# The last FFN of a two-layer kernel: two batches per product of 512 columns, high parts by ScalarE, and the first transposes ahead of the last shared step

## The chip, the cores and the metric

The kernel runs on one core of a Trainium2 chip. The metric is the device time of one execution in microseconds (us); the median of three runs is quoted, and beside it stands one profiled execution, from which every row below comes.

## The reference, cut to what matters

Two layers of cross attention and FFN act on `x` of 4 batches x 256 tokens x 256. The change touches the last FFN, and the order of work at the seam between the mixture-of-experts FFN of the first layer and the attention of the second.

```python
x = x + L0_xattn(layernorm(x), ctx, ...)
x = x + L0_ffn(layernorm(x), ...)              # experts + 0.2 * shared FFN
x = x + L1_xattn(ctx, ctx, masks, layernorm(x), ...)
# L1_ffn on layernorm(x); the weights are lut[idx]
gate = einsum('bsh,oh->bso', x, lut[gate_idx]) # 256 -> 688
up   = einsum('bsh,oh->bso', x, lut[up_idx])   # 256 -> 688
h    = silu(gate) * up
out  = einsum('bsh,oh->bso', h, lut[down_idx]) # 688 -> 256
```

All of it is float32. The kernel gets there on TensorE by splitting both factors in a high and a low part of type fp32r and summing three products (high x high, low x high, high x low).

## The kernel before, in words

Five engines run instruction lists of their own (`@block.tensor` PE, `@block.scalar` ACT, `@block.vector` DVE, `@block.gpsimd` POOL, `@block.sync` SP for DMA), written out by hand in order, and tied by semaphores. Each engine takes its own list strictly in order, so a wait holds up all that stands behind it.

Most of the time goes to ten "units" (the shared FFN in two halves of tokens and eight experts). A unit has nine steps; in each, `first` (L729) makes 6 products into a bank of `hb`, ScalarE applies gelu, and `second` (L748) adds float32 products into `yb` two steps later. The last unit, E + 1, is the second half of the shared FFN; its last two `second` steps stand after the unit.

Then comes the last FFN, the stage of the change. 688 hidden rows are NG = 6 tiles (five of 128, the last of 48, for which gate and up share one product). The four batches of 256 tokens are taken one after another, so that there are 24 tiles n = b * NG + f. The parts are:

- `transpose_x3(b)` (PE, L847): 4 transposes of the normalised rows `xn` into `tb`. It waits for `x3n_ok`. `x3T_copy(b)` (ACT, helper line L902) makes `xT_hi`, and `x3T_split(b)` (DVE, L1519) makes `xT_lo`.
- `gate_up(b, f)` (PE, L868): 6 gate and 6 up products of 256 columns into the two halves of one of four banks (GRING = 4); 6 for the last tile. It waits until the products of the tile four before are taken from the bank (`prod_ok`).
- silu (ACT, L1111 or L1113) of the gate half into `gate_of(r)`.
- two DVE instructions: L1541 writes gate * up as fp32r (`h_hi`), and L1542 writes the same product as float32. POOL (L547) subtracts the two into `h_lo`.
- `down(b, f)` (PE, L883): 6 products of 256 columns into a bank for the batch, three tiles behind gate_up (GLAG = 3).
- `finish(b)` (DVE, L1526) adds the bank to `x`; SP sends the batch to `out`.

Between these tiles the lists of ACT, DVE and POOL carry what is left of the attention for batches 2 and 3 (and the end of batch 1): `combined(b)` (DVE statistics, L1126), `inv_std(3, b)` (POOL, L440 and L433), `attend(b)` (DVE, L1446 to L1457), `exps(1, b)` (ACT, L922, with a change of ScalarE's table to exp and back to silu), `add_probs(1, b, 4)` (DVE, L1272, L1275, L1126), `inv_std(4, b)` (POOL) and `norm_x(4, b)` (DVE, L1132), which releases transpose_x3(b). `add_shared(1)` (DVE, L1431) adds the shared FFN's banks to the tokens of batches 2 and 3, so nothing of these can start before the last `second`.

Of the kernel before, what the change touches and what calls it, by code (L numbers as in the profile page):

```python
# [25 lines left out]
P = 128  # L26
# [22 lines left out]
GRING, GLAG = 4, 3  # L49
# [12 lines left out]
def program(nc, t):  # L62
    xbuf = t["xbuf"]
    ctx = ExitStack()
    with ctx:
# [47 lines left out]
        h_hi = sb("h_hi", [P, GRING, S], F32R)  # L113
        h_lo = sb("h_lo", [P, GRING, S], F32R)
# [59 lines left out]
        ffn_banks = (hb[0], hb[1], hb[2], yb[1])  # L174
# [102 lines left out]
        prod_ok = sem("prod_ok")  # L277
        g_lo_ok = sem("g_lo_ok")
# [138 lines left out]
        def _(gp):  # L417
# [124 lines left out]
            inv_std(4, 0, 1e-5)  # L542

            for n in range(B * NG):
                gp.wait_ge(prod_ok, n + 1)
                r = n % GRING
                gp.tensor_tensor(h_lo[:, r, 0:S], product(r), h_hi[:, r, 0:S].bitcast(F32), ALU.subtract)\  # L547
                    .then_inc(g_lo_ok, 1)
                if n == 0:
                    inv_std(4, 1, 1e-5)  # L550
                elif n == 2:
                    inv_std(3, 2, 1e-5)
                elif n == 5:
                    inv_std(3, 3, 1e-5)
                elif n == 7:
                    inv_std(4, 2, 1e-5)
                elif n == 13:
                    inv_std(4, 3, 1e-5)
# [3 lines left out]
        def _(pe):  # L562
# [272 lines left out]
            for s in range(STEPS - LAG, STEPS):  # L835
                second(E + 1, s, True, 1)

# [13 lines left out]
            def gate_up(b, f):  # L851
                n = b * NG + f
                if n < GRING:
                    if n == GRING - 1:
                        pe.wait_ge(shared_read, 4)
                    pe.wait_ge(h32_ok, UNITS * NF)
                    pe.wait_ge(low_ok, UNITS)
                else:
                    pe.wait_ge(prod_ok, n - GRING + 1)
                if f == 0:  # L860
                    pe.wait_ge(x3T_lo, b + 1)
                last = f == NG - 1
                for part, first_col in enumerate((BOTH0,) if last else (GATE0, UP0)):
                    terms = [(w, a, k) for k in range(DK)
                             for w, a in ((gw_hi, xT_hi), (gw_lo, xT_hi), (gw_hi, xT_lo))]
                    for i, (w, a, k) in enumerate(terms):
                        at = first_col + (k * P if last else k * FULL + f * P)
                        mm = pe.matmul(ffn_banks[n % GRING][:, part * S:(part + 1) * S], w[:, at:at + P],  # L868
                                       a[:, b % 2, k, 0:S], start=(i == 0), stop=(i == len(terms) - 1))
                mm.then_inc(gu_mm, 1)  # L870

            def down(b, f):
                n = b * NG + f
                if n == NG:
                    pe.wait_ge(shared_read, 4)
# [11 lines left out]

            pe.wait_ge(lk, JOBS * JOPS)
            transpose_x3(0)
            for n in range(B * NG + GLAG):  # L890
                if n < B * NG:
                    gate_up(n // NG, n % NG)
                if n >= GLAG:
                    down((n - GLAG) // NG, (n - GLAG) % NG)
                if n % NG == 4 and n // NG + 1 < B:
                    transpose_x3(n // NG + 1)
# [3 lines left out]
        def _(act):  # L900
# [194 lines left out]
            def x3T_copy(b):  # L1095
                act.wait_ge(x3T_mm, b + 1)
                if b >= 2:
                    act.wait_ge(gu_mm, (b - 1) * NG)
                copy(xT_hi[:, b % 2, :, 0:S], tb[b % 2][:, :].rearrange("p (k s) -> p k s", k=DK)).then_inc(x3T_hi, 1)

            x3T_copy(0)
            for n in range(B * NG):
                b, f = n // NG, n % NG
                if n == 6:
                    exps(1, 2)
                elif n == 12:
                    exps(1, 3)
                act.wait_ge(gu_mm, n + 1)
                bank = ffn_banks[n % GRING]
                if f < NG - 1:  # L1110
                    act.activation(gate_of(n % GRING), bank[:, 0:S], ACT.Silu).then_inc(silu_ok, 1)  # L1111
                else:
                    act.activation(gate_of(n % GRING)[0:LASTG, :], bank[H:H + LASTG, 0:S], ACT.Silu).then_inc(silu_ok, 1)  # L1113
                if f == 4 and b + 1 < B:
                    x3T_copy(b + 1)
# [3 lines left out]
        def _(dve):  # L1119
# [392 lines left out]
            unit(E + 1, 1, shared=True, extra=tail)  # L1512
            norm_x(4, 0, x3n_ok)
            add_probs(1, 1, 4, (0,))


            def x3T_split(b):
                dve.wait_ge(x3T_hi, b + 1)
                dve.tensor_tensor(xT_lo[:, b % 2, :, 0:S], tb[b % 2][:, :].rearrange("p (k s) -> p k s", k=DK),  # L1519
                                  xT_hi[:, b % 2, :, 0:S].bitcast(F32), ALU.subtract).then_inc(x3T_lo, 1)  # L1520

            def finish(b):

                dve.wait_ge(down_mm, (b + 1) * NG)
# [8 lines left out]
            for n in range(B * NG):  # L1533
                b, f = n // NG, n % NG
# [91 lines left out]
```

## Time and profile before

| what | us |
|---|---|
| median of 3 runs | 323.04 (321.94 to 325.26) |
| profiled execution, its own time | 322.0 |
| its span | 320.1 |
| PE busy | 301.6 (94%) |
| DVE busy | 239.3 (75%) |
| ACT busy | 153.8 (48%) |
| POOL busy | 104.3 (33%) |

Rows give the start of an instruction in the span, its duration, the engine, the line, the operation, what it writes and reads, and in brackets how long the engine sat idle before and who ended that. Matmuls overlap, so the distance of their starts, and not the duration of one, is what one costs.

### The profile page before, as it was taken

The page shows a single profiled execution, that of the slowest core. Times are in us where ns is not written, and L with a number is a line of the kernel's source. Part 1 is how long each engine was busy: PE and PEld are TensorE (multiplying, and loading weights), DVE is VectorE, ACT ScalarE, POOL GpSimd, SP SyncE. Part 2 cuts the span into 40 slices and gives each one's busy share as a digit, 9 for nine tenths or more (in the row PEclk, how much of TensorE's full clock was granted, in tenths as well). Part 3 has the DMA queues.
Part 4 walks back from the last instruction along what each step waited for, and adds up shares of the span by engine and source line. Part 5 has one row for each costly group of instructions (what it writes and reads, how often), then busy time and mean ns, then how long its engine had stood idle before and what let it go on. Part 6 is the DMA issues. An engine that isn't in the chain of part 4 may idle for free.

```text
span 320.1 us, 5956 instructions
## 1 busy us (share of the span) xinstructions
PE 301.6 (94%) x1913; PEld 257.7 (80%) x1913; DVE 239.3 (75%) x649; ACT 153.8 (48%) x366; POOL 104.3 (33%) x146
## 2 busy tenths in 40 slices
PE   7998779997999999999999999999999979989895
PEld 4654557774989899898989989889888869979795
DVE  4758695602499989898998989899885748796742
ACT  2376473631346465554556555455641833634210
POOL 7327127670000605023060503305052206442432
PEclk9699789999899999999999999999999999999998
DMA  7993114825167574929466492927125000000101
GB/s 223 379 268 74 46 49 121 294 99 158 42 191 246 134 235 80 334 52 273 136 159 204 91 321 58 286 78 187 54 30 143 3 0 2 0 33 2 35 1 66
DMA packets 26258, 41.51 MB, mean 130 GB/s; under 512 B 3898, under 2 KB 16955, under 8 KB 26236
## 3 DMA queue, kind: packets, MB, share of 16 engines
q1 hardware_dynamic: 22012, 36.49, 35.8%
q0 software_dynamic: 4224, 4.75, 8.4%
q8 instruction: 11, 0.18, 0.2%
q14 instruction: 11, 0.09, 0.1%
HBM read 31.40 MB, written 9.82 MB: 129 GB/s over the span
## 4 chain that ended last, share of the span: by engine, by line
PE 83%; DVE 10%; DMA 2%; issue 2%; POOL 2%; SPq 1%; ACT 1%; DVEq 0%; POOLq 0%
PE hb L729 28%; PE yb L748 25%; PE hb L868 8%; PE yb L762 5%; PE tb L660 3%; PE rb L883 3%; PE yb L883 3%; PE yb L868 2%; PE rb L651 1%; POOL rstd L433 1%; DMA projw<-projw_dram 1%; DVE xT_lo L1288 1%; DVE x L1275 1%; PE yb L605 1%; DVE xn L1132 1%
## 5 line engine op out<-in xcount | busy, mean ns | idle before, releaser
L748 PE MATMUL yb<-raw,h 128*128 128x256 f32 x384 | 97.8, 385 | 0.0
L1031 ACT ACTIVATE h<-hb,b 128x320 f32<-128x320 f32 (+1 forms) x80 | 44.6, 559 | 69.9 <-PE hb L729 67.9
L748 PEld LDWEIGHTS yb<-raw,h 128*128 128x128 f32 x384 | 71.0, 194 | 7.6 <-ACT h L1031 0.3
L729 PE MATMUL hb<-xT_hi,w_hi 128*128 128x320 f32 (+1 forms) x180 | 72.4, 402 | 3.3 <-ACT small L1035 1.8
L531 POOL DMA_INDIRECT xacc_dram<-ysb,slot_i x16 | 25.0, 1565 | 126.0 <-ACT ysb L902 123.6
L729 PE MATMUL hb<-xT_lo,w_hi 128*128 128x320 f32 (+1 forms) x180 | 59.5, 331 | 0.0
L729 PE MATMUL hb<-xT_hi,w_lo 128*128 128x320 f32 (+1 forms) x180 | 59.3, 330 | 0.0
L1465 DVE TENSOR_TENSOR w_lo<-raw,w_hi 128x256 fp32r<-128x256 f32 x84 | 34.6, 416 | 17.2 <-ACT w_hi L902 17.1
L1158 DVE COPY_PREDICATED pick<-bits,pick 128x544 int32<-128x544 uint8 x56 | 43.2, 772 | 0.6
L729 PEld LDWEIGHTS hb<-xT_hi,w_hi 128*128 128x128 f32 x180 | 34.4, 191 | 8.9 <-issue 4.3
L729 PEld LDWEIGHTS hb<-xT_hi,w_lo 128*128 128x128 f32 x180 | 34.5, 192 | 2.6
L902 ACT ACTIVATE w_hi<-raw 128x256 fp32r<-128x256 f32 x90 | 36.5, 407 | 0.1
L729 PEld LDWEIGHTS hb<-xT_lo,w_hi 128*128 128x128 f32 x180 | 34.4, 191 | 1.7
L1154 DVE TENSOR_SCALAR pick<-bit,lut_x,lut 128x544 int32<-128x544 int32 x64 | 35.8, 580 | 0.0
L547 POOL TENSOR_TENSOR h_lo<-h,h_hi 128x256 fp32r<-128x256 f32 x24 | 17.7, 742 | 31.9 <-DVE h L1542 31.9
L868 PE MATMUL hb<-xT_hi,gw_hi 128*128 128x256 f32 x68 | 19.6, 288 | 2.9 <-DVE xT_lo L1519 2.8
L1288 DVE TENSOR_TENSOR xT_lo<-tb,xT_hi 128x320 fp32r<-128x320 f32 (+1 forms) x22 | 11.0, 540 | 15.0 <-ACT xT_hi L902 15.0
L868 PE MATMUL hb<-xT_lo,gw_hi 128*128 128x256 f32 x68 | 18.9, 278 | 0.0
L868 PE MATMUL hb<-xT_hi,gw_lo 128*128 128x256 f32 x68 | 18.9, 278 | 0.0
L902 ACT ACTIVATE xT_hi<-tb 128x320 fp32r<-128x320 f32 (+1 forms) x26 | 11.7, 496 | 14.9 <-PE tb L847 8.4
L511 POOL DMA_INDIRECT xbuf_dram<-xn,put_i x16 | 16.1, 1006 | 5.7 <-issue 4.5
L1126 DVE BATCH_NORM_STATS2 bst<-x 128x6 f32<-128x256 f32 x32 | 13.3, 416 | 6.1 <-DMA x<-xacc_dram 2.9
(216 smaller groups left out, 522.5 us busy)
## 6 DMA issues: line engine op xcount, KB each, us to landing
raw<-w1pack_dram SPq DMA_DIRECT2D x30, 384.0 KB, 3.5
raw<-w2pack_dram SPq DMA_DIRECT2D x30, 384.0 KB, 5.2
xbuf_dram<-h SPq DMA_DIRECT2D x8, 323.8 KB, 9.5
idx<-idx_dram SPq DMA_DIRECT2D x8, 272.0 KB, 6.0
xg<-xbuf_dram SPq DMA_DIRECT2D x8, 259.0 KB, 6.0
x<-x_dram SPq DMA_DIRECT2D x4, 256.0 KB, 4.5
xacc_dram<-x SPq DMA_DIRECT2D x2, 512.0 KB, 8.8
x<-xacc_dram SPq DMA_DIRECT2D x4, 256.0 KB, 4.0
```

The lines of the kernel that those rows point to most:

```text
L511: gp.indirect_dma_start(rows, bass.IndirectOffsetOnAxis(ap=put_i[:, tile, k:k + 1], axis=0), xn[:, tile, :], None, bounds_check=E * SLOTS ...
L531: gp.indirect_dma_start(t["xacc"], bass.IndirectOffsetOnAxis(ap=slot_i[:, u % 3, c:c + 1], axis=0), ysb[:, c, :], None, compute_op=ALU.add ...
L547: gp.tensor_tensor(h_lo[:, r, 0:S], product(r), h_hi[:, r, 0:S].bitcast(F32), ALU.subtract)\
L729: mm = pe.matmul(hb[s % RING][:, 0:n], w[:, s, k * P:(k + 1) * P], a[:, turn, k, 0:n], start=(i == 0), stop=(i == len(terms) - 1))
L748: mm = pe.matmul(yb[c // 2][:, (c % 2) * D:(c % 2 + 1) * D], h, w, start=(s == 0 and c % 2 == 0), stop=(s == STEPS - 1), skip_group_check= ...
L868: mm = pe.matmul(ffn_banks[n % GRING][:, part * S:(part + 1) * S], w[:, at:at + P], a[:, b % 2, k, 0:S], start=(i == 0), stop=(i == len(te ...
L883: mm = pe.matmul(down_banks[b % 2][:, i * D:(i + 1) * D], h[0:K, n % GRING, i * P:(i + 1) * P], w[0:K, at:at + D], start=(f == 0 and i == ...
L902: return act.activation(dst, src, ACT.Copy, scale=scale)
L1031: act.activation(hidden(s - 1, shared, turn), bank[:, 0:n], ACT.Gelu, bias=b1[:, expert, s - 1:s])\
L1154: dve.tensor_scalar(dst, bit0[:, :], lut_x[:, n:n + 1], lut_i[:, 2 * n:2 * n + 1], ALU.bitwise_and, ALU.bitwise_xor).then_inc(lk, 1)
L1158: dve.copy_predicated(dst, m, src).then_inc(lk, 1)
L1465: dve.tensor_tensor(w_lo[:, slot, :], raw1[:, slot, :], w_hi[:, slot, :].bitcast(F32), ALU.subtract)\
```

## The change

Batches are taken in two pairs. In each pair the f-th tile of both batches is one group g of 12 (g = pair * 6 + f); gate products go to one bank and up products to another, two banks each, with 512 columns (2 batches x 256). The group f = 0 still makes products of 256 columns, first those of the even batch, then those of the odd one. The tiles n = 0 to 23 now alternate between the batches of a pair. DVE makes the product once, in float32; its fp32r copy is made by ScalarE (`product_hi`). `h_hi` and `h_lo` now lie in the memory of `w_hi` and `w_lo`, in a ring of six. `down` follows two groups behind. `transpose_x3(0)` stands ahead of the last `second` of the shared FFN and `transpose_x3(1)` right behind it; those of batches 2 and 3 stand behind the down products of g = 4 and g = 5. DVE's order at the seam changes, and so do the places of the attention's remaining pieces.

In the diff, cut to its core, a chain of `if n == ...` is written as `n == 0: ...`, and `...` marks what is left out.

```diff
-GRING, GLAG = 4, 3
+GRING, GLAG = 6, 2
+PAIRS, HALVES = B // 2, 2 * NG
-        ffn_banks = (hb[0], hb[1], hb[2], yb[1])
+        gate_banks, up_banks = (hb[0], hb[2]), (hb[1], yb[1])
+        h_hi, h_lo = w_hi, w_lo
 @@ POOL
+            inv_std(4, 1, 1e-5)
+            for n in range(PAIRS * HALVES):
+                gp.wait_ge(g_hi_ok, n + 1)
+                h_lo[n % 6] = product - h_hi          (gp.tensor_tensor, then g_lo_ok)
+                n == 1: inv_std(3, 2)   n == 3: inv_std(3, 3)
+                n == 6: inv_std(4, 2)   n == 9: inv_std(4, 3)
 @@ PE
+            def gate_up(g):
+                p, f = g // NG, g % NG
+                if g < 2:
+                    pe.wait_ge(h32_ok, UNITS * NF)
+                    pe.wait_ge(low_ok, UNITS)
+                    if g == 1:
+                        pe.wait_ge(shared_read, 4)
+                else:
+                    pe.wait_ge(prod_ok, 2 * g - 2)
+                for cols in (slice(0, S), slice(S, 2 * S)) if f == 0 else (slice(0, 2 * S),):
+                    if f == 0:
+                        pe.wait_ge(x3T_lo, 2 * p + 1 + cols.start // S)
+                    for bank, first_col in ((gate_banks[g % 2], BOTH0),) if last else ((gate_banks[g % 2], GATE0),
+                                                                                       (up_banks[g % 2], UP0)):
+                        for i, (w, a, k) in enumerate(terms):
+                            at = first_col + (k * P if last else k * FULL + f * P)
+                            mm = pe.matmul(bank[:, cols], w[:, at:at + P], a[:, p, k, cols],
+                                           start=(i == 0), stop=(i == len(terms) - 1))
+            for s in range(STEPS - LAG, STEPS - 1):
+                second(E + 1, s, True, 1)
+            transpose_x3(0)
+            second(E + 1, STEPS - 1, True, 1)
+            transpose_x3(1)
             pe.wait_ge(lk, JOBS * JOPS)
+            for g in range(PAIRS * NG + GLAG):
+                if g < PAIRS * NG:
+                    gate_up(g)
+                if g >= GLAG:
+                    down(2 * (g - GLAG))
+                    down(2 * (g - GLAG) + 1)
+                if g in (4, 5):
+                    transpose_x3(g - 2)
 @@ ACT
+            def product_hi(n):
+                act.wait_ge(prod_ok, n + 1)
+                if n >= GRING:
+                    act.wait_ge(down_mm, n - GRING + 1)
+                copy(h_hi[0:K, r, :], product(r)[0:K, :]).then_inc(g_hi_ok, 1)
+            x3T_copy(0)
+            x3T_copy(1)
+            for n in range(0, PAIRS * HALVES, 2):
+                if n == 4:
+                    exps(1, 2)
+                elif n == 8:
+                    exps(1, 3)
+                silu(n)
+                silu(n + 1)
+                product_hi(n)
+                product_hi(n + 1)
+                if n in (8, 10):
+                    x3T_copy(n // 2 - 2)
 @@ DVE
-            norm_x(4, 0, x3n_ok)
             add_probs(1, 1, 4, (0,))
+            norm_x(4, 0, x3n_ok)
+            add_probs(1, 1, 4, (1,))
+            norm_x(4, 1, x3n_ok)
+            x3T_split(0)
             for later in range(2, B):
                 dve.wait_ge(x_back[later], 16)
             add_shared(1)
-            x3T_split(0)
+            x3T_split(1)
+            for n in range(PAIRS * HALVES):
+                dve.wait_ge(silu_ok, n + 1)
-                dve.tensor_tensor(h_hi[0:K, r, 0:S], gate_of(r)[0:K, :], up, ALU.mult)
                 dve.tensor_tensor(product(r)[0:K, :], gate_of(r)[0:K, :], up, ALU.mult).then_inc(prod_ok, 1)
+                n == 0: combined(2)        n == 1: attend(2)
+                n == 2: combined(3)        n == 3: attend(3)
+                n == 5: add_probs(1, 2, 4) n == 7: norm_x(4, 2, x3n_ok)
+                n == 8: add_probs(1, 3, 4) n == 9: x3T_split(2)
+                n == 10: norm_x(4, 3, x3n_ok)
+                n == 11: x3T_split(3)
+                n == 15: finish(0), finish(1)
+            finish(2)
+            finish(3)
```

## Rows read from the trace of the kernel before

**Rows 1.** The page: granted clock in 40 slices of 8 us, and the chain's shares.
```profile
PEclk9699789999899999999999999999999999999998
...
PE 83%; DVE 10%; DMA 2%; issue 2%; POOL 2%; SPq 1%; ACT 1%; DVEq 0%; POOLq 0%
```

**Rows 2.** Chain that ended last, 250 us on: start us, us, what.
```profile
249.91 1.40 PE hb L729 x6
...
259.95 1.29 DVE x L1431 x2
...
261.98 4.33 PE hb L868 x36
...
287.12 1.65 PE hb L868 x12
...
304.26 1.38 PE yb L868 x12
305.64 0.71 PE rb L883 x6
...
316.81 0.69 DVE x L1526
```

**Rows 3.** Instructions of DVE in order of time, 256 to 284 us.
```profile
256.17 0.73 DVE L1132 TENSOR_SCALAR xn<-x,mv,rstd 128x256 f32<-128x256 f32 x2 [1.13 <-POOL rstd L433]
...
264.05 0.42 DVE L1541 TENSOR_TENSOR h_hi<-h,hb 128x256 fp32r<-128x256 f32 x1 [2.21 <-ACT h L1111]
264.39 0.41 DVE L1542 TENSOR_TENSOR h<-h,hb 128x256 f32<-128x256 f32 x1
...
268.74 0.41 DVE L1126 BATCH_NORM_STATS2 bst<-x 128x6 f32<-128x256 f32 x1
...
269.81 0.39 DVE L1541 TENSOR_TENSOR h_hi<-h,yb 128x256 fp32r<-128x256 f32 x1
...
272.21 1.00 DVE L1446 SCALAR_TENSOR_TENSOR xg<-x,mv,scores 128x256 f32<-128x256 f32 x2
...
274.83 0.41 DVE L1541 TENSOR_TENSOR h_hi<-h,hb 48x256 fp32r<-48x256 f32 x1
...
279.26 0.16 DVE L1272 RECIPROCAL rsum<-esum 128x2 f32<-128x2 f32 x1
...
282.11 0.40 DVE L1541 TENSOR_TENSOR h_hi<-h,hb 128x256 fp32r<-128x256 f32 x1
...
283.33 1.13 DVE L1132 TENSOR_SCALAR xn<-x,mv,rstd 128x256 f32<-128x256 f32 x2 [0.48 <-POOL rstd L433]
```

**Rows 4.** Instructions of ACT in order of time, 263 to 293 us.
```profile
263.63 0.38 ACT L1111 ACTIVATE h<-hb 128x256 f32<-128x256 f32 x1 [1.46 <-PE hb L868]
...
274.93 0.60 ACT L922 ACTIVATE xg<-xg,nmx,rstd 128x256 f32<-128x256 f32 x1 [1.57 <-DVE nmx L1457]
...
276.22 1.28 ACT L1111 ACT_TABLE_LOAD   x1
...
292.30 1.07 ACT L1111 ACTIVATE h<-hb 128x256 f32<-128x256 f32 x3
```

**Rows 5.** The page: ScalarE's copies of 128x256 to fp32r, mean ns.
```profile
L902 ACT ACTIVATE w_hi<-raw 128x256 fp32r<-128x256 f32 x90 | 36.5, 407 | 0.1
```

**Rows 6.** Instructions of POOL in order of time, 278 to 283 us.
```profile
278.76 1.42 POOL L547 TENSOR_TENSOR h_lo<-h,h_hi 128x256 fp32r<-128x256 f32 x2 [1.01 <-DVE h L1542]
282.29 0.22 POOL L440 TENSOR_SCALAR vare<-mv 128x2 f32<-128x2 f32 x1 [2.10 <-DVE mv L1129]
```

**Rows 7.** Instructions of PE in order of time that began after idle time.
```profile
34.13 0.71 PE L676 MATMUL rb<-xT_hi,gate_parts 128*128 128x512 f32 x2 [2.65 <-DVE xT_lo L1288]
...
284.51 0.66 PE L847 MATMUL tb<-ident,xn 128*128 128x128 f32 x4 [0.97 <-DVE xn L1132]
```

**Rows 8.** Windows: stretch, length, busy (x) of PE, PEld, DVE, ACT, POOL, clock, DMA, GB/s.
```profile
34.00:36.00 2.00, 1.87 (x6) 1.51 (x7) 1.75 (x8) 0.33 (x1) 0.00 (x0) 0.70 0.00 0
36.00:38.00 2.00, 2.00 (x6) 1.18 (x4) 0.00 (x0) 1.86 (x7) 1.36 (x2) 0.50 0.00 0
```

More of the change, by code:

```diff
@@ L542, in _ @@
             inv_std(4, 0, 1e-5)
-            for n in range(B * NG):
-                gp.wait_ge(prod_ok, n + 1)
+            inv_std(4, 1, 1e-5)
+            for n in range(PAIRS * HALVES):
+                gp.wait_ge(g_hi_ok, n + 1)
                 r = n % GRING
-                gp.tensor_tensor(h_lo[:, r, 0:S], product(r), h_hi[:, r, 0:S].bitcast(F32), ALU.subtract)\
+                gp.tensor_tensor(h_lo[:, r, :], product(r), h_hi[:, r, :].bitcast(F32), ALU.subtract)\
                     .then_inc(g_lo_ok, 1)
-                if n == 0:
-                    inv_std(4, 1, 1e-5)
-                elif n == 2:
+                if n == 1:
                     inv_std(3, 2, 1e-5)
-                elif n == 5:
+                elif n == 3:
                     inv_std(3, 3, 1e-5)
-                elif n == 7:
+                elif n == 6:
                     inv_std(4, 2, 1e-5)
-                elif n == 13:
+                elif n == 9:
                     inv_std(4, 3, 1e-5)
@@ L862, in gate_up @@
                 last = f == NG - 1
[L863 to L869, printed above, removed]
+                for cols in (slice(0, S), slice(S, 2 * S)) if f == 0 else (slice(0, 2 * S),):
[3 more added lines that the diff above has]
+                                                                                       (up_banks[g % 2], UP0)):
+                        terms = [(w, a, k) for k in range(DK)
+                                 for w, a in ((gw_hi, xT_hi), (gw_lo, xT_hi), (gw_hi, xT_lo))]
+                        for i, (w, a, k) in enumerate(terms):
+                            at = first_col + (k * P if last else k * FULL + f * P)
+                            mm = pe.matmul(bank[:, cols], w[:, at:at + P], a[:, p, k, cols],
+                                           start=(i == 0), stop=(i == len(terms) - 1))
@@ L870, in gate_up, with down @@
                 mm.then_inc(gu_mm, 1)
[L872 to L874 removed]
+            def down(n):
+                b, f = n // HALVES * 2 + n % 2, n // 2 % NG
+                if n == 1:
                     pe.wait_ge(shared_read, 4)
@@ L1542, in _ @@
                 dve.tensor_tensor(product(r)[0:K, :], gate_of(r)[0:K, :], up, ALU.mult).then_inc(prod_ok, 1)
-                if f == 4 and b + 1 < B:
-                    x3T_split(b + 1)
                 if n == 0:
-                    add_probs(1, 1, 4, (1,))
-                elif n == 1:
-                    norm_x(4, 1, x3n_ok)
-                elif n == 2:
                     dve.wait_ge(shared_read, 4)
                     combined(2)
-                elif n == 4:
+                elif n == 1:
@@ L1553, in _ @@
                     attend(2)
+                elif n == 2:
+                    combined(3)
+                elif n == 3:
+                    attend(3)
                 elif n == 5:
-                    combined(3)
+                    add_probs(1, 2, 4)
                 elif n == 7:
-                    add_probs(1, 2, 4)
+                    norm_x(4, 2, x3n_ok)
                 elif n == 8:
-                    norm_x(4, 2, x3n_ok)
+                    add_probs(1, 3, 4)
+                elif n == 9:
+                    x3T_split(2)
@@ L1560, in _ @@
                 elif n == 10:
-                    attend(3)
-                elif n == 13:
-                    add_probs(1, 3, 4)
-                elif n == 14:
                     norm_x(4, 3, x3n_ok)
-                if f == 3 and b > 0:
-                    finish(b - 1)
-            finish(B - 1)
+                elif n == 11:
+                    x3T_split(3)
+                elif n == 15:
+                    finish(0)
+                    finish(1)
+            finish(2)
+            finish(3)
```

65 lines of the change are left out of this document (20 added, 45 removed).

## The prediction

> **What bounds the kernel now.** I read the page first: the chain that ended last is TensorE for 83% of the span and DVE for 10% [rows 1]. So TensorE bounds the kernel, and the question for the changed stage is how long it stands still there. Next I read the chain from 250 us on. The last FFN begins with gate_up at 261.98 and its last products release the last finish at 316.81 [rows 2], 54.8 us. TensorE's own work in it comes from two rows of that chain: 12 gate/up products of 256 columns take 1.38 (0.115 each) and 6 down products 0.71 (0.118 each) [rows 2]. There are 264 of the first and 144 of the second, 30.3 + 17.0 = 47.3 us, and three sets of transposes of about 0.4 each (the set at 284.51 is followed by a matmul at 284.92), 1.2. That leaves about 6 us in which TensorE waits or restarts, in many small pieces. The longest idle stretch of the stage is about 1 us: 0.97 ahead of the transposes of batch 2 [rows 7]. The granted clock stays at nine tenths or more through the stage [rows 1]. DVE's list, with two product instructions per tile and the attention of batches 2 and 3 between them, is what TensorE waits for at these places.
>
> **The wider products.** 216 of the 264 gate/up products merge into 108 of 512 columns; the 48 of the two groups f = 0 stay. The same kind of product with 512 columns stands in the shared FFN: 6 in 1.40 us, 0.233 each [rows 2]. So 108 x 0.233 = 25.2 us takes the place of 216 x 0.115 = 24.8: a loss of 0.4 us, not a gain. The halved weight loads are worth nothing, since they overlap the matmuls already. The Trainium skill ("TensorE: Matmul & The Clock Gate", section "Wait — 56ns, not 53.3ns?") gives each warm matmul a fixed cost of about 2.5 ns on top of its columns; merging would then save 108 x 2.5 ns = 0.3 us. The rows here disagree with it for this operand type, and I go by them. Either way it is less than 0.5 us: TensorE's work stays at 48.6 us, and the time is decided by its waits.
>
> **The start.** Before, batch 0's split waits behind the addition of the shared banks (259.95, 1.29 us), and gate_up starts at 261.98 [rows 2]. After, DVE does half of add_probs(1, 1) in its idle 1.13 us ahead of norm_x(4, 0) [rows 3], the other half (1.2) to 258.1, waits about 1.1 for the root from POOL and normalises batch 1 (0.73) to 259.9. The split of batch 0 needs none of the last shared step: it ends near 260.5, and gate_up starts near 260.7, when TensorE has done both transposes (the last shared step ends 0.4 later, at about 260.1). The addition then runs 260.5 to 261.8 and batch 1's split to 262.4, so the second half of group 0 starts at 262.5 and ends at 263.9. In the old order the same work (two tiles and the second transposes) would be done at 261.98 + 2.8 + 0.4 = 265.2. The gain is 1.3 us.
>
> **What is late next: one chain through ACT, DVE and POOL.** TensorE cannot begin batch 2 before norm_x(4, 2), nor batch 3 before norm_x(4, 3), and gate_up(g) needs the products of group g - 2. I follow the lists in order with these durations. Silu starts 0.2 after the group's slot on TensorE ends, and DVE 0.42 after silu starts (263.63 to 264.05) [rows 3, 4]. A product takes 0.41 and lets the next start after 0.34; combined takes 1.07 (268.74 to 269.81), attend 2.62 (272.21 to 274.83), add_probs 2.85 (279.26 to 282.11) [rows 3]. exps are two table loads of 1.28 and 1.29 between them (274.93 to 276.22), 3.85 in all [rows 4]; back-to-back silus are 0.35 apart (three in 1.07) [rows 4]. A ScalarE copy for the high part is the same shape as w_hi, 0.41 [rows 5]. POOL's subtraction takes 0.71 (two in 1.42), and from the start of inv_std to norm_x is 1.04 (282.29 to 283.33) [rows 3, 6].
>
> - Products 0 to 3: 264.1 + 0.42 = 264.5; combined(2), product 1 at 265.9; attend(2), product 2 at 268.9; combined(3), product 3 from 270.3 to 270.7. ACT's high part 3 ends at 271.1. Only then, in ACT's order, come exps(1, 2), though their input was ready at 268.9: silu 4 starts at 275.0, and product 5 ends at 276.2.
> - TensorE meanwhile: group 1 (2.8) to 266.7, group 2 to 269.5, down (1.4) to 270.9, group 3 to 273.7, down to 275.1. Group 4 waits for product 5: idle 1.2. It ends at 279.1, its down products at 280.5.
> - add_probs(1, 2) 276.1 to 278.9, products 6 and 7 to 279.7. POOL reaches inv_std(4, 2) only behind the subtraction of tile 6, near 280.6; norm_x(4, 2) 281.6 to 282.8. TensorE is idle for 2.3. Transposes, group 5, down: to 286.1.
> - High part 7 ends at 280.2, exps(1, 3) delay silu 8 to 284.05. Product 8 at 284.5, add_probs(1, 3) to 287.7, product 9 to 288.1, high part 9 to 288.5, x3T_copy(2) to 289.1, then silu 10 and split(2), product 10 to 290.1, norm_x(4, 3) to about 291.4. TensorE has been idle since 286.1: 5.3 us.
> - Transposes of batch 3 to 291.8, group 6 with a short wait for the second split to 294.8. From here TensorE isn't waited on: down 1.4, four groups with their down products 4 x 4.2 = 16.9, the last group 1.4, and six more tiles of down 4.3 give 318.8. The group ring holds: each product has over 4 us.
>
> Before, the finish starts at 316.81; now at about 319.0: 2.2 us later. The work sums to the same: start -1.3, wider products +0.4, and 1.2 + 2.3 + 5.3 + 0.3 of idle time in place of about 6.
>
> **The end.** Two batches now finish within 0.7 us of one another (0.69 per finish [rows 2]), so the last output transfer has another beside it. No row shows that pair; the one alone takes 320.1 - 317.5 = 2.6. The bounds are nothing and 2.6 in a row; each is 256 KB, and half of them overlap anyway: I take 0.3.
>
> **The clock.** At 34.13 TensorE came back from 2.65 us idle [rows 7]; the clock stood at 0.70 of full in the next 2 us and 0.50 in those after [rows 8], so 2 x 0.30 + 2 x 0.50 = 1.6 us of work was lost. In the 8 us slice from 8 us on it was 0.6 [rows 1], 3.2 us lost. In the stage before, with idle stretches of 1 us, nothing was lost. The new idle stretch of 5.3 us follows one of 2.3, and everything behind it hangs on TensorE. I bound the cost by 0 and 3.2 and take 1.8, near the 1.6 of the one stretch of known idle time, with a little for the longer idle. (Where it falls after the 2.3 us stretch it costs nothing, since TensorE then waits anyway.) The Trainium skill (same page, section "What's actually happening") says that the slow state is the default and that activity releases it; by that rule the engine comes back from 5.3 us at 1.2 GHz and stays there for a while. The row at 34.13 agrees.
>
> **Smaller edits.** DVE loses 24 product instructions of 0.34, 8 us of its list; ScalarE gains 24 copies of 0.41, 10 us of a list that is short: three silus stand in a row at 292.30 because it had fallen behind only for the exps [rows 4]. Neither is a term of its own: they are in the chain. h_hi and h_lo in older memory cost nothing, because their readers are done when the last gelu has run, which group 0 waits for anyway. SP's list is unchanged.
>
> **The sum.** 2.2 + 0.3 + 1.8 = 4.3 us. Against the profiled execution's own time, 322.0, that is 326.3; the median of the runs shown is 1.0 above it, so 323.04 + 4.3 = 327.3 us, 1.3% slower.
>
> **Rivals.**
> - The waits come as worked out, and the clock holds, as it did through 1 us gaps: +2.5, 325.5 us. Against it speaks the row at 34.13. Chance 0.20.
> - The chain is shorter than my sum (it has over 25 links, some of them waits for POOL, and DVE's two-input instructions vary between 0.48 and 1.0 us): the wait for batch 3 shrinks by 2.5 us and the clock drops little. Then about 323. Chance 0.15.
> - The other side: the DVE instructions removed are what mattered. If the rows of batch 3 are normalised by 286.1, TensorE never waits for batches 2 and 3; then 1.3 + about 5 of the old 6 us fall away, less 0.4 and 0.3: -5.6 to -6.5, about 317. It decides at one point: norm_x(4, 3) has to come 5.3 us earlier than I find, which would take exps(1, 3) off ACT's path altogether. Chance 0.08.
> - Worse: the slow clock takes 3.2 and the chain is 1 us longer: 330. Chance 0.07.
>
> My forecast holds the remaining 0.50, with its own range 325.5 to 329.5.
>
> **How the numbers follow.** About 1% is what a measurement of this kernel can tell from no change (319.8 to 326.3 us). Faster by over 1%: the third rival, 0.08. Within 1%: most of the first rival (0.15), the second (0.13), and a fifth of the forecast (0.10), 0.38 with the rounding. Slower: 0.54. The range 322.5 to 330.0 leaves out the third rival and the far ends, about 0.15 to 0.2.
>
> **What would show it.** Right: an idle stretch of TensorE of about 5 us ahead of the transposes of batch 3, ended by DVE's xn, another of about 2 us ahead of those of batch 2, about 1 us ahead of group 4; 512-column products at 0.233; a clock below 1.00 in the 4 us behind the long stretch; the first gate_up near 260.7; ACT's table load for exp right behind the high part of tile 3. Wrong: transposes of batch 3 right behind the down products; 512-column products at under 0.22; a finish of the last batch before 316.8.

## The result and the profile after

The changed kernel takes 331.48 us (median of 20 runs, 324.95 to 335.89); the kernel before took 325.09 in the same rounds (20 runs, 321.87 to 331.72). The ratio is 1.0137, 95% interval 1.0099 to 1.0175: 1.4% slower. The ratio leaves out disturbed executions, some per cent longer whatever the kernel: ten of the 20 of the changed kernel, whose other ten have a median of 329.1.

The page of the changed kernel, with the lines that answer to [rows 1]; the clock row has one digit for each of 40 slices.

```profile
span 327.0 us, 5751 instructions
...
PEclk9699799998799999999999999999999999997998
...
PE 62%; DVE 17%; issue 5%; POOL 5%; DMA 4%; ACT 4%; another core or an unknown queue 1%; SPq 1%; POOLq 0%; DVEq 0%
```

TensorE's share of the chain that ended last fell from 83% to 62%, and DVE, POOL and ACT took most of it (13% before, 26% now): a part of the time now hangs on them. The clock has a new dip, a 7, in the slice at 294 us.

Spans can't be compared directly. Of the 6.9 us between the two spans, 3.0 lie ahead of everything that the change touches: between 72 and 107 us TensorE waited 2.4 us for an expert's rows from DMA in one execution and 0.2 in the other. So I measure from a mark that no edit touches, the first down products of the last unit (`w_up` into `yb`), to the end of the span, and call this the stretch. First, in the kernel before, the mark and the first gate_up.

```profile
238.17 0.63 PE L748 MATMUL yb<-w_up,lowrank 128*128 128x256 f32 x4
...
261.98 0.36 PE L868 MATMUL hb<-xT_hi,gw_hi 128*128 128x256 f32 x1 [1.74 <-DVE xT_lo L1519]
```

Then TensorE's instructions of the changed kernel, in order of time: the mark, the first gate_up, and the three that began after idle time.

```profile
241.17 0.63 PE L748 MATMUL yb<-w_up,lowrank 128*128 128x256 f32 x4
...
263.38 0.36 PE L868 MATMUL hb<-xT_hi,gw_hi 128*128 128x256 f32 x1
...
279.37 0.50 PE L868 MATMUL hb<-xT_hi,gw_hi 128*128 128x512 f32 x1 [1.04 <-DVE h L1567]
...
285.95 0.66 PE L844 MATMUL tb<-ident,xn 128*128 128x128 f32 x4 [2.11 <-DVE xn L1154]
...
294.12 0.77 PE L844 MATMUL tb<-ident,xn 128*128 128x128 f32 x4 [4.69 <-DVE xn L1154]
```

The stretch was 320.1 - 238.17 = 81.93 us and is 327.0 - 241.17 = 85.83: 3.9 us longer, within the interval of the whole time (1.0137 x 325 is +4.4). The three idle stretches are where the forecast put them: 1.04, 2.11 and 4.69 us, against 1.2, 2.3 and 5.3. Before, the two ahead of the transposes of batches 2 and 3 were 0.97 [rows 7] and 1.04 us; the longest of the stage was the 1.74 us ahead of the first gate_up, which the prediction overlooked, and which is gone in the changed kernel. The first gate_up comes 22.2 us after the mark; before, 261.98 - 238.17 = 23.8 [rows 2].

What held the third one back is in ScalarE's list (the same kernel, in order of time):

```profile
272.43 0.42 ACT L908 ACTIVATE w_hi<-h 128x256 fp32r<-128x256 f32 x1 [2.17 <-DVE h L1567]
273.82 0.42 ACT L908 ACTIVATE w_hi<-h 128x256 fp32r<-128x256 f32 x1 [0.97 <-DVE h L1567]
274.26 1.28 ACT L928 ACT_TABLE_LOAD   x1
...
276.85 1.28 ACT L1113 ACT_TABLE_LOAD   x1
278.14 0.66 ACT L1113 ACTIVATE h<-hb 128x256 f32<-128x256 f32 x2
...
290.69 0.42 ACT L908 ACTIVATE w_hi<-h 128x256 fp32r<-128x256 f32 x1 [2.22 <-DVE h L1567]
291.01 0.58 ACT L908 ACTIVATE xT_hi<-tb 128x512 fp32r<-128x512 f32 x1
```

The high parts of tiles 2 and 3 wait 2.17 and 0.97 us for DVE's product, and only then comes the table load for exp. Silu 4 starts at 278.14; group 4 waits for it. At 290.69 the high part of tile 9 has waited 2.22 us, and the copy of batch 2's transposes, written by 286.6, stands behind it. DVE's normalisations of batches 2 and 3 follow at the end of these links, each behind a root from POOL:

```profile
284.77 1.13 DVE L1154 TENSOR_SCALAR xn<-x,mv,rstd 128x256 f32<-128x256 f32 x2 [1.95 <-POOL rstd L434]
...
292.92 1.14 DVE L1154 TENSOR_SCALAR xn<-x,mv,rstd 128x256 f32<-128x256 f32 x2 [0.29 <-POOL rstd L434]
```

The windows of the changed kernel around the long gap (columns as in [rows 8]) show the clock:

```profile
292.00:294.00 2.00, 0.00 (x0) 0.00 (x0) 1.71 (x5) 0.68 (x2) 1.55 (x3) 1.00 0.00 0
294.00:296.00 2.00, 1.88 (x11) 1.89 (x12) 0.83 (x3) 1.02 (x2) 0.74 (x1) 0.63 0.00 0
296.00:298.00 2.00, 2.00 (x11) 2.00 (x11) 0.25 (x1) 0.00 (x0) 0.00 (x0) 0.51 0.00 0
298.00:300.00 2.00, 2.00 (x19) 2.00 (x18) 0.43 (x2) 0.66 (x2) 0.00 (x0) 1.00 0.00 0
```

0.51 of full is the lower of the two levels, 1.2 GHz; by these windows it lasted about 3.4 us ((0.37 + 0.49) x 2 / 0.5), behind 4.69 us without a matmul.

Last, the chain of the changed kernel in a warm part of the second pair, and its end:

```profile
313.59 2.80 PE hb L868 x12
316.38 0.71 PE rb L884 x6
317.10 0.71 PE yb L884 x6
...
323.70 0.69 DVE x L1552
```

Twelve products of 512 columns take 2.80, 0.233 each as in the shared FFN [rows 2]; two tiles of twelve 256-column products took 2 x 1.38. The last finish ends at 324.39, 2.6 us ahead of the end of the span, as before: with a second output transfer beside it the end took no longer.

### The profile page after: what moved, and what is told of

Read it like the earlier page. It is cut to its first block, busy times and chain, and to the rows that moved or that the text cites. A ratio compares the mean times of both kernels' runs of the same rounds, so it can differ in the third digit from the quotient of the medians.

```text
span 327.0 us, 5751 instructions
## 1 busy us (share of the span) xinstructions
PE 301.9 (92%) x1805; PEld 253.8 (78%) x1805; DVE 231.0 (71%) x625; ACT 161.9 (50%) x390; POOL 105.3 (32%) x146
## 4 chain that ended last, share of the span: by engine, by line
PE 62%; DVE 17%; issue 5%; POOL 5%; DMA 4%; ACT 4%; another core or an unknown queue 1%; SPq 1%; POOLq 0%; DVEq 0%
PE hb L729 22%; PE yb L748 19%; PE hb L868 5%; PE yb L762 5%; PE tb L660 3%; DVE bst L1148 3%; DVE x L1297 2%; PE rb L884 2%; POOL rstd L434 2%; PE yb L884 2%; POOL xbuf_dram L512 1%; DVE xn L1154 1%; DVE mv L1151 1%; DMA xacc_dram<-ysb,slot_i 1%; DMA projw<-projw_dram 1%
## 5 line engine op out<-in xcount | busy, mean ns | idle before, releaser
L532 POOL DMA_INDIRECT xacc_dram<-ysb,slot_i x16 | 25.0, 1565 | 126.8 <-ACT ysb L908 124.4
L729 PEld LDWEIGHTS hb<-xT_hi,w_hi 128*128 128x128 f32 x180 | 34.4, 191 | 8.9 <-issue 3.9
L729 PEld LDWEIGHTS hb<-xT_lo,w_hi 128*128 128x128 f32 x180 | 34.4, 191 | 1.8
L549 POOL TENSOR_TENSOR w_lo<-h,w_hi 128x256 fp32r<-128x256 f32 x24 | 18.2, 769 | 37.8 <-ACT w_hi L908 37.8
L1567 DVE TENSOR_TENSOR h<-h,hb 128x256 f32<-128x256 f32 (+1 forms) x16 | 6.2, 413 | 17.1 <-ACT h L1113 15.0
L868 PE MATMUL hb<-xT_hi,gw_hi 128*128 128x512 f32 (+1 forms) x44 | 17.0, 386 | 1.2 <-DVE h L1567 1.0
L535 POOL DMA_INDIRECT xacc_dram<-ysb,slot_i x8 | 15.5, 1940 | 2.4 <-issue 2.4
```

The source lines that it names most:

```text
L532: gp.indirect_dma_start(t["xacc"], bass.IndirectOffsetOnAxis(ap=slot_i[:, u % 3, c:c + 1], axis=0), ysb[:, c, :], None, compute_op=ALU.add ...
L549: gp.tensor_tensor(h_lo[:, r, :], product(r), h_hi[:, r, :].bitcast(F32), ALU.subtract)\
L729: mm = pe.matmul(hb[s % RING][:, 0:n], w[:, s, k * P:(k + 1) * P], a[:, turn, k, 0:n], start=(i == 0), stop=(i == len(terms) - 1))
L868: mm = pe.matmul(bank[:, cols], w[:, at:at + P], a[:, p, k, cols], start=(i == 0), stop=(i == len(terms) - 1))
```

## The experiments

All stretches in one table, each from the trace of one execution (the seam alone was traced twice, with 79.88 and 80.04), so a difference of a few tenths of a us rests on one pair of traces. The spans of e1 (327.3), e4 (330.9) and e8 (323.5) are long ahead of the mark, which stands there at 247.42, 245.80 and 243.46; the stretches leave that out. In e1 and e8 the clock reads 1.00 in every window of the stage up to TensorE's last product, as in the kernel before. "Batch 3" is the start of its transposes behind the mark.

| kernel | stretch | against before | idle ahead of batches 2 / 3 | batch 3 at | from there to the end |
|---|---|---|---|---|---|
| before | 81.93 | 0 | 0.97 / 1.04 | 61.1 | 20.8 |
| changed | 85.83 | +3.90 | 2.11 / 4.69 | 52.95 | 32.88 |
| e1, e8: seam alone | 79.88, 80.04 | -2.0 | 0.92 / 1.07 | | |
| e2: gap filled | 84.78 | +2.85 | 2.11 / 0.53 | 53.08 | 31.70 |
| e3: both exps together | 82.75 | +0.82 | 2.23 / 2.87 | 50.03 | 32.72 |
| e4: high parts on DVE | 85.10 | +3.17 | 2.01 / 2.11 | 52.13 | 32.97 |
| e6: halves of 256 | 86.13 | +4.20 | 2.12 / 3.15 | 53.10 | 33.03 |
| e7: exps ahead of high parts | 84.46 | +2.53 | 2.18 / 2.91 | 50.33 | 34.13 |
| e5: changed kernel, reordered | 78.65 | -3.28 | 0.56 / 0.67 | | |
| e9: kernel before, seam and order | 77.28 | -4.65 | none / none | | |

In the kernel before batch 3 comes after the other three are nearly done, so its two last columns aren't comparable with those of the pairs.

**The seam alone (e1_seam and e8_seam).**

```diff
-            for s in range(STEPS - LAG, STEPS):
-                second(E + 1, s, True, 1)
...
-            transpose_x3(0)
+            second(E + 1, STEPS - 2, True, 1)
+            transpose_x3(0)
+            second(E + 1, STEPS - 1, True, 1)
...
+            x3T_split(0)
             for later in range(2, B):
                 dve.wait_ge(x_back[later], 16)
             add_shared(1)
-            x3T_split(0)
```

> The kernel before with the seam alone: transposes of batch 0 ahead of the last shared step and its split ahead of the addition of the shared banks. First theory (each part has the price worked out ahead of the result): gate_up starts right behind the last shared step, about 1 us earlier against that step than before, and the stage ends up to 1 us earlier if DVE's list isn't the bound behind it: ratio 0.997 to 1.000. Rival (the seam costs something, by the split or the transposes in between): ratio above 1.002.

TensorE around the end of the last shared step, in order of time (e1_seam):

```profile
247.42 0.63 PE L748 MATMUL yb<-w_up,lowrank 128*128 128x256 f32 x4
...
267.11 0.60 PE L843 MATMUL tb<-ident,xn 128*128 128x128 f32 x4
267.55 1.89 PE L748 MATMUL yb<-raw,h 128*128 128x256 f32 x8
269.21 0.36 PE L864 MATMUL hb<-xT_hi,gw_hi 128*128 128x256 f32 x1
```

The first gate_up follows the last down product of the shared step with no gap, 21.79 us behind the mark instead of 23.81, and the stretch is 2.0 us shorter: the 1.74 us of idle time that stood there before are gone. All of it is kept: the FFN's own length, from the first to the last product, is 54.55 us against 54.52. I had expected half of that. The whole times of this run gave no ratio, so the kernel ran again.

> The kernel before with the seam alone once more, for its whole time (in its first run the stage began its products 2.0 us earlier against the last unit than in the kernel before, and kept all of it to the end). First theory (the seam is worth 2 us by itself, and the change then loses 6 in the stage): ratio 0.992 to 0.996. Rival (the gain of that one trace was chance): 0.998 to 1.002.

The whole time gave 0.9966 (0.9915 to 1.0017): consistent with -2 us, and with nothing. The second trace gave -1.9. So the traces carry this, not the times.

**The gap filled (e2_fill).**

```diff
                 if g >= GLAG:
                     down(2 * (g - GLAG))
                     down(2 * (g - GLAG) + 1)
+                if g == 5:
+                    keep_busy(38, tb[1])
                 if g in (4, 5):
                     transpose_x3(g - 2)
```

> The changed kernel with 38 idle products of 256 columns in the long gap of TensorE, ahead of the transposes of batch 3. They take about 4.1 us of the 4.7 us gap and change nothing that is computed. First theory (the clock falls because TensorE stands still there, and its low stretch is a cost of its own): the granted clock stays at 1.00 behind the gap, gate_up of group 6 runs at 0.115 per product, and the end comes 1.5 us earlier than in the changed kernel: ratio to before about 1.009. Rival (the clock's fall costs nothing, since the waits behind cover it, or it falls in any case): no change, ratio 1.013 to 1.014.

```profile
239.12 0.63 PE L748 MATMUL yb<-w_up,lowrank 128*128 128x256 f32 x4
...
284.04 0.66 PE L844 MATMUL tb<-ident,xn 128*128 128x128 f32 x4 [2.11 <-DVE xn L1156]
...
292.20 0.66 PE L844 MATMUL tb<-ident,xn 128*128 128x128 f32 x4 [0.53 <-DVE xn L1156]
```

The transposes of batch 3 come at the same place (53.08 behind the mark against 52.95), since DVE's chain sets them. The clock reads 1.00 in every window from there to TensorE's last product, and from them to the end it takes 31.70 us against 32.88. So the low clock costs 1.2 us in the traced execution of the changed kernel, as a cost of its own. The whole times point to more: the ratio to before is 1.0029 (0.9985 to 1.0073), not the 1.009 that I expected, and against 1.0137, from other rounds, that is some 3.5 us. The mean granted clock of the executions compared was 0.976 to 0.984 with the gap filled and 0.955 to 0.971 in the changed kernel (0.966 in the traced one). So the low clock may cost more in other executions, as it does in e7_link below; no trace of the changed kernel shows one.

**Both exps together (e3_exps).**

```diff
-                if n == 4:
-                    exps(1, 2)
-                elif n == 8:
-                    exps(1, 3)
                 silu(n)
                 silu(n + 1)
+                if n == 4:
+                    exps(1, 2)
+                    exps(1, 3)
```

> The changed kernel with ScalarE's two exps moved: both stand together behind silu 4 and silu 5, so two of the four table loads go, and group 4 needn't wait. First theory (the order of ScalarE's list sets the idle stretches of TensorE): idle ahead of group 4 falls from 1.0 to under 0.3 us, the stretch ahead of the transposes of batch 3 shrinks from 4.7 to about 3 to 4, and the end comes 2 to 3 us earlier than in the changed kernel: ratio 1.004 to 1.008. Rival (DVE's work sets them, and the place of the exps doesn't matter): idle stretches as in the changed kernel, ratio 1.012 to 1.015.

```profile
239.05 0.63 PE L748 MATMUL yb<-w_up,lowrank 128*128 128x256 f32 x4
...
282.70 0.66 PE L844 MATMUL tb<-ident,xn 128*128 128x128 f32 x4 [2.23 <-DVE xn L1153]
...
289.08 1.11 PE L844 MATMUL tb<-ident,xn 128*128 128x128 f32 x4 [2.87 <-DVE xn L1153]
```

The idle stretch ahead of group 4 is gone, that of batch 3 is 2.87, and the stretch is 3.1 us shorter than in the changed kernel. The first theory's numbers held within 0.2 us; its rival, under which the idle stretches stay, fell. Two table loads went too, so this run alone doesn't tell the place of the exps from the number of the loads. The few whole times (ratio 1.011, 0.998 to 1.024) don't decide.

**High parts on DVE (e4_dvehi).**

```diff
+                if n >= GRING:
+                    dve.wait_ge(down_mm, n - GRING + 1)
+                dve.tensor_tensor(h_hi[0:K, r, :], gate_of(r)[0:K, :], up, ALU.mult)
                 dve.tensor_tensor(product(r)[0:K, :], gate_of(r)[0:K, :], up, ALU.mult).then_inc(prod_ok, 1)
...
-                product_hi(n)
-                product_hi(n + 1)
...
-                gp.wait_ge(g_hi_ok, n + 1)
+                gp.wait_ge(prod_ok, n + 1)
```

> The changed kernel with the high parts back on DVE: two product instructions per tile as before, no copy by ScalarE. First theory (high parts by ScalarE shorten DVE's list by 0.34 per tile and put 0.4 us links into the chain at tiles 3, 7 and 9): the chain to the transposes of batch 3 gets about 3.7 us of DVE and loses about 1.3 us of links, so the stage is about 2 us longer than in the changed kernel: ratio about 1.02. Rival (the copies on ScalarE are what makes the change slow): the stage gets shorter, ratio 1.005 or less.

The first theory missed: I had expected 2 us more than in the changed kernel; it is 0.7 less. The rival had the direction and the ratio (1.005 or less) right, but 0.7 of 3.9 us doesn't make the copies the cause of the loss. ScalarE's list of this kernel (its mark stands at 245.80) shows why:

```profile
274.54 0.66 ACT L1113 ACTIVATE h<-hb 128x256 f32<-128x256 f32 x2 [2.14 <-PE yb L868]
275.22 1.28 ACT L928 ACT_TABLE_LOAD   x1
277.63 0.60 ACT L928 ACTIVATE xg<-xg,nmx,rstd 128x256 f32<-128x256 f32 x1 [1.13 <-DVE nmx L1477]
```

The table load for exp stands right behind silu 3, 29.4 us after the mark; in the changed kernel it came at 274.26, 33.1 after it. The exp itself then waits 1.13 us for its input from DVE and starts 31.8 after the mark, against 34.4. A high part in ScalarE's list costs not its 0.42 us but the wait for DVE's product ahead of it, and all that is queued behind pays. That wait is what DVE's 0.34 us per tile was traded for, and the trade was about even: batch 3 begins 0.8 us earlier with the high parts on DVE (52.13 against 52.95). The whole time's ratio to before is 1.0053 (0.9995 to 1.0111).

**Exps ahead of the high parts (e7_link),** to test that reading with everything else kept.

```diff
-                if n == 4:
-                    exps(1, 2)
-                elif n == 8:
-                    exps(1, 3)
                 silu(n)
                 silu(n + 1)
+                if n == 2:
+                    exps(1, 2)
+                elif n == 6:
+                    exps(1, 3)
```

> The changed kernel with exps(1, 2) ahead of the high parts of tiles 2 and 3, and exps(1, 3) ahead of those of tiles 6 and 7, with all four table loads kept. Theory formed from the run with the high parts on DVE (a high part in ScalarE's list costs not its 0.4 us but the wait for DVE's product in front of it, which holds back the exps that stand behind): the first exps start about 3 us earlier against the last unit, no idle ahead of group 4, under 2 us ahead of the transposes of batch 2 and about 3.6 ahead of those of batch 3, the end 3 to 4 us earlier than in the changed kernel: ratio 1.000 to 1.005. Rival (the place of the exps matters only through the table loads, two of which the run with both exps together had saved): at most 1 us earlier, ratio 1.010 or more.

```profile
266.26 1.28 ACT L928 ACT_TABLE_LOAD   x1
268.07 0.60 ACT L928 ACTIVATE xg<-xg,nmx,rstd 128x256 f32<-128x256 f32 x1 [0.53 <-DVE nmx L1479]
```

Its mark stands at 236.74, so the table load comes 29.5 us behind it, 3.6 earlier, and the exp 31.3 behind it, 3.0 earlier, since it waits 0.53 us for its own input. No idle ahead of group 4 is left, and the transposes of batch 3 begin 2.6 us earlier than in the changed kernel: the link is there, with all four table loads kept. But the stretch is only 1.4 us shorter, because this execution lost more to the clock (windows of e7_link):

```profile
286.00:288.00 2.00, 0.93 (x5) 0.93 (x6) 1.34 (x3) 0.45 (x2) 0.88 (x2) 0.56 0.00 0
288.00:290.00 2.00, 2.00 (x11) 2.00 (x11) 0.69 (x1) 0.60 (x1) 0.60 (x1) 0.50 0.00 0
290.00:292.00 2.00, 2.00 (x11) 2.00 (x11) 0.00 (x0) 0.00 (x0) 0.00 (x0) 0.50 0.00 0
292.00:294.00 2.00, 2.00 (x15) 2.00 (x14) 0.29 (x1) 0.66 (x2) 0.00 (x0) 0.74 0.00 0
```

About 6.8 us at the lower level around an idle stretch of 2.91, and 34.13 us from batch 3 to the end against 31.70 with the gap filled: 2.4 us. The idle time ahead of batch 2 didn't shrink, which I had expected to be under 2: inv_std(4, 2) stands behind the subtraction of tile 6, and that now waits for exps(1, 3). The few whole times gave 1.0254 (1.0104 to 1.0405), slower than the stretch says. That lies outside the theory's ratio and inside the rival's (1.010 or more); the 1.4 us of the stretch lie between the two. Only the earlier start of the chain is shown here, by the trace; what the whole times hold beside the stretch stays open.

**Halves of 256 columns in every group (e6_halves).**

```diff
-                for cols in (slice(0, S), slice(S, 2 * S)) if f == 0 else (slice(0, 2 * S),):
+                for cols in (slice(0, S), slice(S, 2 * S)):
```

> The changed kernel with every group's products in two halves of 256 columns (first those of the even batch, then those of the odd one), all else as it is: 264 products of 256 columns in place of 108 of 512 and 48 of 256. First theory (a 512-column product costs 0.233, twice 256 costs 0.230): the same time within 0.4 us, ratio 1.012 to 1.014, distance of starts 0.115. Rival (512 columns save a fixed cost per product): 0.3 us or more longer than the changed kernel, and a distance of starts above 0.1165.

The chain of this kernel in the warm part, the same group as above:

```profile
305.47 2.83 PE hb L868 x24
308.30 0.71 PE rb L884 x6
```

24 products take 2.83 where 12 wide ones took 2.80: equal within 0.03 us per group, 0.3 in ten groups, and the stretch is 0.3 longer. The distance is 0.118, above the 0.1165 that the rival named, so both of the rival's signs came, the first just at its bound: wide products gain about 0.3 here and don't lose 0.4. One trace can't settle 0.3 us, and this kernel's clock fell in another place (last section); what is shown is that the width moves the time by no more than a few tenths. The whole times of this kernel were too scattered for a ratio.

**The changed kernel, reordered (e5_order).** Nothing is added or taken away but two table loads.

```diff
-                elif n == 6:
+                elif n == 5:
                     inv_std(4, 2, 1e-5)
...
+                    if g == NG and cols.start:
+                        between()
...
-                if g in (4, 5):
-                    transpose_x3(g - 2)
+                if g == 4:
+                    transpose_x3(2)
...
+                if n != 4:
+                    silu(n)
+                    silu(n + 1)
+                else:
+                    exps(1, 2)
+                    exps(1, 3)
+                product_hi(n)
+                if n == 2:
+                    silu(4)
+                    silu(5)
+                product_hi(n + 1)
...
-                elif n == 8:
-                    add_probs(1, 3, 4)
                 elif n == 9:
+                    add_probs(1, 3, 4, (0,))
                     x3T_split(2)
-                elif n == 10:
-                    norm_x(4, 3, x3n_ok)
+                    add_probs(1, 3, 4, (1,))
                 elif n == 11:
+                    norm_x(4, 3, x3n_ok)
                     x3T_split(3)
```

`between()` is down(8), transpose_x3(3), down(9), and stands between the two halves of group 6.

> The changed kernel with its lists put in another order, nothing else: silu 4 and 5 ahead of the high part of tile 3, both exps together behind it (two table loads fewer), inv_std(4, 2) two tiles earlier, products 8 and 9 ahead of add_probs(1, 3), split(2) between its halves, products 10 and 11 ahead of norm_x(4, 3), and the transposes of batch 3 between the two halves of group 6. First theory (the wider grouping is sound, and only the order of the lists costs): idle stretches of TensorE of 1 us or less, about 1.5 us in all, the clock at 1.00 throughout, the end about 5 us earlier than before: ratio about 0.984. Rival (two batches at a time with two banks each can't be fed, whatever the order): idle stretches of 2 us or more remain, ratio 1.00 or above.

```profile
238.15 0.63 PE L748 MATMUL yb<-w_up,lowrank 128*128 128x256 f32 x4
...
280.32 0.66 PE L844 MATMUL tb<-ident,xn 128*128 128x128 f32 x4 [0.56 <-DVE xn L1164]
...
286.59 0.66 PE L844 MATMUL tb<-ident,xn 128*128 128x128 f32 x4 [0.67 <-DVE xn L1164]
...
288.66 0.39 PE L875 MATMUL hb<-xT_hi,gw_hi 128*128 128x256 f32 x1 [0.69 <-DVE xT_lo L1555]
```

Ratio 0.9856 (0.9793 to 0.9920); the stretch is 7.2 us shorter than in the changed kernel and 3.3 shorter than before (I had said 5). The clock reads 1.00 in every window of the stage up to TensorE's last product. Two batches at a time can be fed; the order of the lists, with the two table loads that go with it, was the cost.

**The kernel before with the seam and one edit of order (e9_oldorder).** Beside the seam's diff:

```diff
-                elif n == 7:
+                elif n == 6:
                     inv_std(4, 2, 1e-5)
-                elif n == 13:
+                elif n == 12:
                     inv_std(4, 3, 1e-5)
...
                 elif n == 5:
                     combined(3)
-                elif n == 7:
                     add_probs(1, 2, 4)
-                elif n == 8:
+                elif n == 7:
                     norm_x(4, 2, x3n_ok)
                 elif n == 10:
                     attend(3)
-                elif n == 13:
+                elif n == 11:
                     add_probs(1, 3, 4)
-                elif n == 14:
+                elif n == 13:
                     norm_x(4, 3, x3n_ok)
```

> The kernel before, one batch at a time, with the seam and one more edit of order: add_probs(1, 2) and add_probs(1, 3) stand two tiles earlier in DVE's list, norm_x(4, 2), norm_x(4, 3) and their inv_std one tile earlier. First theory (the grouping by two batches brings nothing by itself; what the reordered changed kernel gained is seam and order): the idle stretches of 0.9 to 1.1 us ahead of the transposes of batches 2 and 3 go, the end comes 4 us earlier than before, ratio 0.985 to 0.990, as good as the reordered changed kernel. Rival (DVE's 24 further products bind the old form): ratio 0.992 or more.

TensorE around the transposes of batch 2 (its mark stands at 238.52):

```profile
281.75 0.28 PE L879 MATMUL yb<-gw_lo,h_hi 128*128 128x256 f32 x1
281.87 0.60 PE L843 MATMUL tb<-ident,xn 128*128 128x128 f32 x4
282.22 0.37 PE L864 MATMUL yb<-xT_hi,gw_hi 128*128 128x256 f32 x1
```

The transposes follow with no gap; waits of 0.44 and 0.27 us for the two splits are left. Ratio 0.9893 (0.9849 to 0.9936), and the shortest stretch of all, 77.28, 1.4 us below the reordered pairs. By the whole times the two can't be told apart. DVE's 24 further products, which the change took away, don't bind this order. Both versions beat both kernels.

## Why the prediction was right, step by step

The forecast was +4.3 us (327.3 us, 1.3% slower), from three terms; measured were +3.9 in the stretch and a ratio of 1.0137. On the median shown ahead of the prediction the ratio gives 1.0137 x 323.04 = 327.5. The plain median of 331.48 lies above the range's 330.0; the 329.1 of the executions that the ratio compares lies within it.

- **The wider products, +0.4.** Right in kind, too large in size. 0.233 for 512 columns held exactly, but in the same place of the same kernel 24 narrow ones take 2.83, not 2.76. Against those the wide ones save 0.03 us per group, where I had a loss of 0.04; and 47.3 + 1.2 + 0.4 is 48.9, not 48.6. The Trainium skill's fixed cost per warm matmul ("TensorE: Matmul & The Clock Gate", section "Wait — 56ns, not 53.3ns?") would make 24 against 12 products 0.03 us, an estimate from its figure. The 0.03 seen agrees with it, against my reading of the rows, though 0.233 is above the 0.216 that the section gives for 512 columns.
- **The start, -1.3.** The first gate_up came 1.6 earlier and the first group ended 1.5 earlier, the second half waiting for its split as worked out. What I missed is the 1.74 us of idle time ahead of the old first gate_up: the seam alone takes it away and gives 2.0 when it needn't wait for batch 1's transposes.
- **The chain through ACT, DVE and POOL.** Each link came in order. Batch 3's transposes were forecast at 291.4 - 238.17 = 53.2 behind the mark and came at 52.95. The idle stretches came as 1.04 + 2.11 + 4.69 = 7.8 for a forecast of 8.8. Reordering, with two table loads fewer, gave 7.2 us of the stretch back (e5), putting both exps together gave 3.1 (e3), and moving them with all loads kept brought batch 3 forward by 2.6 (e7): the chain is shown, not argued.
- **Its reading in one place was incomplete.** "Smaller edits" named the copies as links of 0.41 us; e4 and e7 show that a link's price is the wait for DVE that it puts ahead of the exps: at tiles 2 and 3 it holds back the table load by about 3.6 us and the exp by 2.5 to 3.0. The sum had it, since I followed the lists in order, but the expectation for e4 went wrong by 2.7 us for lack of it.
- **Behind batch 3.** I had 27.6 us from there to the last finish's start with a warm clock; e2 shows 31.70 - 3.3 = 28.4. About half of the 0.8 are restarts that I counted as nothing: in the chain of the changed kernel some groups with their down products take 4.42 us (300.53 to 304.95) and others 4.22 (313.59 to 317.81), and the extra 0.2 is 0.10 each at two first products (303.27 and 304.88); what holds those isn't shown. The finish without the clock's part came 2.7 us later than before, not 2.2.
- **The end, +0.3.** Nothing: 2.6 us as before.
- **The clock, +1.8.** It fell where forecast; the price in the traced execution of the changed kernel is 1.2 (e2), and 2.4 in e7_link's, so 1.8 is inside what traces show. It was taken from a stretch near the start of the kernel, so that it comes out near is partly luck.

The errors +0.5, -0.3 and -0.6 nearly cancelled, so the total is nearer than its terms; that closeness is luck. Of the rivals, the one in which the clock holds fell with the window at 0.51. The one on the other side fell as it was drawn (DVE's removed instructions don't matter while ScalarE's exps hold the chain), and once the order was mended the grouping beat the kernel before by 3.3 us, not by 5.6 to 6.5; e9 shows that this gain needs no grouping. The rival with the shorter chain fell too: the wait for batch 3 came 0.6 shorter than forecast, not 2.5. The worse case (3.2 for the clock) shows in no trace.

## What to carry to other kernels

When an instruction moves to an idle engine, price not its duration but the wait that it brings into that engine's list, and look at what is queued behind it: here two copies of 0.4 us delayed exp's table load by 3.6 us and the exp by 2.5 to 3.0. Before regrouping work, walk each engine's list once with the new waits; seam and order mended in the old form gave 4.7 us of the stretch, more than the new form with its own order mended (3.3). A gap of several us in TensorE can also cost clock behind it (1.2 and 2.4 us here), so a late operand may be paid for twice.

## What the runs showed of the hardware

- The clock's fall isn't a fixed price. After idle stretches of 4.69 and 2.91 us the low level lasted about 3.4 and 6.8 us, at 1.2 and 2.4 us of lost time: the shorter gap cost more; in e3_exps, after 2.87, it lasted 3.4 (0.68, 0.50 and 0.97 in three windows from 288 us on). And 2.11 us of idle time ahead of batch 2 left the clock at 1.00 in the changed kernel and in e2_fill, as did 2.23 in e3_exps and 2.18 in e7_link, but in e6_halves, with 2.12, it read 0.76, 0.50 and 0.88 in the 6 us behind (in e4_dvehi, with 2.01, 0.50 and 0.65 in four). The Trainium skill ("TensorE: Matmul & The Clock Gate", section "What's actually happening") has the slow state as the default that activity lifts; the runs agree, and show that the same gap may or may not bring it on. The windows of e6_halves around that gap:

```profile
276.00:278.00 2.00, 0.20 (x2) 0.21 (x3) 1.12 (x2) 1.97 (x6) 1.27 (x2) 1.00 0.00 0
278.00:280.00 2.00, 2.00 (x15) 2.00 (x14) 0.51 (x3) 1.78 (x4) 0.00 (x0) 0.76 0.00 0
280.00:282.00 2.00, 2.00 (x12) 2.00 (x11) 1.88 (x5) 0.32 (x1) 0.73 (x1) 0.50 0.00 0
```

- A normalisation of two tiles on DVE takes 0.73 us alone [rows 3], 1.13 with one POOL subtraction beside it, and 1.71 and 1.55 in e5_order, where two subtractions in a row (1.48 from 278.64, 1.47 from 284.91) ran beside them. So the normalisation is longer by 0.4 to 0.5 us for each POOL subtraction beside it, while two of POOL's take little more than the 1.42 of [rows 6]; no run here isolates the cause.
